# A transformer layer on one core: the first and last rounds written out by hand, the values' bias folded into the output bias, warm-up matmuls at the start

## What is computed

```python
def attn(x):                                   # after _layernorm(x)
    Q = jnp.einsum('btd,hkd->bthk', x, W_Q) + b_Q      # K, V alike
    scores = jnp.einsum('bqhk,bshk->bhqs', Q, K) / sqrt(d_head)
    attn = jax.nn.softmax(scores, axis=-1)
    out_h = jnp.einsum('bhqs,bshk->bqhk', attn, V)
    return jnp.einsum('bqhk,hdk->bqd', out_h, W_O) + b_O
def ffn(x):                                    # after _layernorm(x)
    gate = softmax(xt @ gate_w.T)
    base = xt @ weight.T
    t = jnp.einsum('nh,erh->ner', xt, lora_U)
    return base + jnp.einsum('ne,eor,ner->no', gate, lora_V, t) / 16
x = x + _layernorm(attn(_layernorm(x)))
x = x + _layernorm(ffn(_layernorm(x)))
```

## Time and profile before

| | us |
|---|---|
| median of 3 runs | 1220.18 (1218.62 to 1221.35) |
| the profiled execution's own time | 1221.85 |
| its span, first to last instruction | 1220.0 |
| granted TensorE clock, mean | 0.990 |
| PE busy | 1185.9 (97%) |
| DVE, ACT, POOL busy | 958.6, 967.9, 728.3 |

### The profile page before, as it was taken

The page is one execution under the profiler, slowest core; times in us unless marked ns, Lnnn a source line. Parts: engine busy times, 40 slices in busy tenths (PEclk is TensorE's granted clock), DMA queues, the critical chain, the costliest instruction groups (busy, mean ns, idle before and its releaser), DMA issues.

```text
span 1220.0 us, 32981 instructions
## 1 busy us (share of the span) xinstructions
PE 1185.9 (97%) x10532; PEld 977.1 (80%) x10532; DVE 958.6 (79%) x2618; ACT 967.9 (79%) x3079; POOL 728.3 (60%) x946
## 2 busy tenths in 40 slices
PE   6899999999999999999999999999999999999995
PEld 3688888888888888888888888888888888888883
DVE  4677888887888887887877878877888878788883
ACT  2678888888888888888888888888888888888882
POOL 2556556665556665566665666675556665555653
PEclk9899999999999999999999999999999999999997
DMA  6000000000000000000000000000000000000000
GB/s 213 2 1 6 2 6 4 4 4 4 0 4 4 4 4 4 0 4 4 4 4 4 4 0 4 4 4 4 4 0 4 4 4 4 4 0 4 4 4 9
DMA packets 9923, 10.95 MB, mean 9 GB/s; under 512 B 816, under 2 KB 9392, under 8 KB 9904
## 3 DMA queue, kind: packets, MB, share of 16 engines
q1 hardware_dynamic: 9904, 10.70, 2.7%
HBM read 6.50 MB, written 4.19 MB: 9 GB/s over the span
## 4 chain that ended last, share of the span: by engine, by line
PE 82%; POOL 7%; DVE 6%; issue 4%; ACT 1%; POOLq 0%; DVEq 0%; DMA 0%; SPq 0%; ACTq 0%
PE o_ps L383 17%; PE st_ps L365 17%; PE st_ps L355 14%; PE extra_ps L398 8%; PE qk_ps L304 4%; PE qk_ps L306 4%; PE qk_ps L305 4%; POOL probs L1021 3%; PE extra_ps L337 3%; PE extra_ps L339 2%; PE extra_ps L338 2%; DVE probs_t L806 2%; PE extra_ps L270 2%; POOL xn L1010 1%; POOL xn L1015 1%
## 5 line engine op out<-in xcount | busy, mean ns | idle before, releaser
L1021 POOL TENSOR_TENSOR probs<-probs,inv_sum 128x512 f32<-128x512 f32 x512 | 525.4, 1042 | 352.6 <-DVE inv_sum L801 342.0
L563 ACT ACTIVATE probs<-st_ps,neg_max 128x256 f32<-128x256 f32 x1024 | 475.2, 482 | 102.6 <-DVE neg_max L794 99.7
L794 DVE TENSOR_REDUCE neg_max<-st_ps 128x2 f32<-128x512 f32 x512 | 332.0, 680 | 48.8 <-PE st_ps L355 45.7
L365 PE MATMUL st_ps<-ident,probs 128*128 128x128 f32 x2048 | 286.6, 275 | 6.7 <-POOL probs L1021 5.1
L365 PEld LDWEIGHTS st_ps<-ident,probs 128*128 128x128 f32 x2048 | 233.9, 141 | 46.9 <-POOL probs L1021 21.6
L383 PE MATMUL o_ps<-probs_t,v_sb 128*64 128x256 f32 x2048 | 256.3, 387 | 0.3 <-DVE o_lo L812 0.2
L563 ACT ACTIVATION_READ_ACCUMULATOR probs<-st_ps,neg_max 128x1 f32 x1024 | 217.1, 212 | 0.0
L806 DVE COPY probs_t<-st_ps 128x512 f32<-128x512 f32 x256 | 169.4, 683 | 37.4 <-PE st_ps L365 37.3
L383 PEld LDWEIGHTS o_ps<-probs_t,v_sb 128*64 128x64 f32 x2048 | 133.4, 136 | 73.2 <-issue 5.9
L778 DVE TENSOR_TENSOR qk_lo<-qk_ps,qk_hi 128x512 fp32r<-128x512 f32 x256 | 175.1, 684 | 11.8 <-ACT qk_hi L550 11.5
L571 ACT COPY probs_t<-st_ps 128x512 f32<-128x512 f32 x256 | 152.5, 596 | 32.6 <-PE st_ps L365 32.6
(11 more groups left out here) (116 smaller groups left out, 2073.4 us busy)
## 6 DMA issues: line engine op xcount, KB each, us to landing
out<-x_all SPq DMA_DIRECT2D x32, 128.0 KB, 1.7
x_all<-in_x SPq DMA_DIRECT2D x1, 3840.0 KB, 17.3
stage_v<-in_w_v SPq DMA_DIRECT2D x1, 512.0 KB, 4.1
stage_o<-in_w_o SPq DMA_DIRECT2D x1, 512.0 KB, 6.7
stage_q<-in_w_q SPq DMA_DIRECT2D x1, 384.0 KB, 4.7
stage_k<-in_w_k SPq DMA_DIRECT2D x1, 384.0 KB, 5.8
x_all<-in_x SPq DMA_DIRECT2D x2, 128.0 KB, 3.1
ffn<-in_ffn_w SPq DMA_DIRECT2D x1, 196.0 KB, 6.8
```

Source lines behind the costliest of these rows:

```text
L365: last = nc.tensor.transpose(st_ps[p % 2][h][:, s * T + j * P:s * T + (j + 1) * P], probs[p % N_PROBS][h][:, j, s * P:(s + 1) * P], ident[ ...
L563: last = nc.scalar.activation(probs[n][h][:, j, :], st_ps[p % 2][h][:, j * T:(j + 1) * T], ACT.Exp, bias=neg_max[n][h][:, j:j + 1], accum_ ...
L794: nc.vector.tensor_reduce(neg_max[p % N_PROBS][h][:, :], st_ps[p % 2][h][:, :].rearrange("p (j s) -> p j s", j=NT), AX.X, ALU.max, negate= ...
L1021: nc.gpsimd.tensor_tensor(probs[n][h][:, :, :], probs[n][h][:, :, :], inv_sum[n][h][:, :].unsqueeze(2).to_broadcast([P, NT, T]), ALU.mult) ...
```

## The change

It has four parts.

1. `body` loses its `live` tests and is only used inside the loop, in the same order as before; `run` keeps only the loop. What body(0) to body(2) did before the loop, and body(32) and body(33) after it, is written out on every engine in a new order. Rounds 0 to 2 still reach the same point before the loop.
2. The bias of V is no longer put on the weights. W_V is used as loaded (pieces 2 and 3 of `MEANS` and the diagonals for v go away). Instead `ffn_means` multiplies W_V with a column of ones (8 matmuls of one column), DVE forms `v_offset`, and `output_bias` (9 matmuls of one column) carries it through W_O into the output bias.
3. PE runs 12 fp32 matmuls of 128 x 128 (`warm_up`) before its first real work.
4. ACT starts with a copy of one column (`seen_one`), so its table load comes early; stats_x(1) and stats_x(2) move to the front of DVE's list. The loads, and their order on SP, do not change.

```diff
+WARM_UPS = 12
@@ tensor @@
+            def warm_up():
+                for _ in range(WARM_UPS):
+                    nc.tensor.matmul(st_ps[1][1][:, 0:P], mean_w[:, :], mean_w[:, :], start=True, stop=True)
+            def ffn_means():
+                pe.wait_ge(mean_folded, 5)
+                pe.wait_ge(ffn_rows_centred, 1)
+                nc.tensor.matmul(o_ps[:, 0:D + TG], mean_w[:, :], ffn[:, F_W:F_W + D + TG],
+                                 start=True, stop=True)
+                pe.wait_ge(w_loaded["v"], 16)
+                for pair in range(PAIRS):
+                    last = nc.tensor.matmul(o_ps[:, D + TG + pair:D + TG + pair + 1],
+                                            stage["v"][:, pair_cols(pair)], one[:, 0:1],
+                                            start=True, stop=True)
+            def output_bias():
+                pe.wait_ge(v_offset_ready, 1)
+                pe.wait_ge(ffn_ready, 1)
+                pe.wait_ge(w_o_centred, 1)
+                dst = o_ps[:, D + TG + PAIRS:D + TG + PAIRS + 1]
+                nc.tensor.matmul(dst, neg_mean_w[:, :], bias[:, B_O:B_O + 1], start=True, stop=False)
+                for pair in range(PAIRS):
+                    last = nc.tensor.matmul(dst, stage["o"][:, pair_cols(pair)], v_offset[:, pair:pair + 1],
+                                            start=False, stop=(pair == PAIRS - 1))
@@ PE before the loop @@
+            warm_up()
+            weight_means(0)
+            transpose_xn(0)
+            weight_means(1)
+            weight_means(2)
+            project_v(0, 0, free=(xt_lo_ready, 1))
+            project_qk(0, 0)
+            project_qk(0, 1)
+            weight_means(3)
+            project_v(0, 1, free=(v_copied[0], 1))
+            weight_means(4)
+            scores(0, 0)
+            weight_means(5)
+            project_v(0, 2, free=(v_copied[1], 1))
+            ffn_means()
+            scores(0, 1)
+            transpose_probs(0, 0, 1, free=(exp_ready[1], 1))
+            project_qk(0, 2, free=(qk_lo_ready, 1))
+            project_qk(0, 3, free=(qk_lo_ready, 2))
+            output_bias()
+            transpose_probs(0, 0, 0, free=(exp_ready[0], 1))
...
+            project_qk(0, 7, free=(qk_lo_ready, 6))
+            probs_v(0, 0)
+            probs_v(0, 1)
+            transpose_probs(0, 2, 1, free=(exp_ready[1], 3))
+            transpose_probs(0, 2, 0, free=(exp_ready[0], 3))
+            transpose_probs(0, 3, 1, free=(exp_ready[1], 4))
...
+            scores(1, 0, free0=(probs_t_copied[0], 7), free1=(probs_t_copied[1], 7))
+            project_qk(1, 4, free=(qk_lo_ready, 11))
+            scores(1, 1, free0=(probs_t_copied[0], 8), free1=(probs_t_copied[1], 8))
+            project_qk(1, 5, free=(qk_lo_ready, 12))
+            probs_v(0, 6, free=(o_lo_ready, 3))
+            probs_v(0, 7)
+            transpose_probs(1, 0, 1, free=(exp_ready[1], 9))
+            transpose_probs(1, 0, 0, free=(exp_ready[0], 9))
+            transpose_probs(1, 1, 1, free=(exp_ready[1], 10))
...
+            scores(1, 5, free0=(probs_t_copied[0], 12), free1=(probs_t_copied[1], 12))
+            transpose_x1(0, free=(x1_ready, 1))
+            transpose_probs(1, 4, 0, free=(exp_ready[0], 13))
+            transpose_xn(2, free=(x1t_ready, 1))
+            transpose_probs(1, 4, 1, free=(exp_ready[1], 13))
+            project_qk(2, 0, free=(qk_lo_ready, 15))
...
+            probs_v(1, 6, free=(o_lo_ready, 7))
+            probs_v(1, 7)
+            transpose_probs(2, 0, 0, free=(exp_ready[0], 17))
+            output_projection(1, 0, free=(v_copied[2], 3))
...
+            transpose_probs(2, 3, 1, free=(exp_ready[1], 20))
+            scores(2, 4, free0=(probs_t_copied[0], 19), free1=(probs_t_copied[1], 19))
+            scores(2, 5, free0=(probs_t_copied[0], 20), free1=(probs_t_copied[1], 20))
+            transpose_x1(1, free=(x1_ready, 2))
+            transpose_probs(2, 4, 0, free=(exp_ready[0], 21))
@@ PE after the loop @@
             run(pe, 2, body)
+            transpose_probs(31, 4, 1, free=(exp_ready[1], 253))
+            probs_v(31, 2, free=(o_lo_ready, 125))
+            probs_v(31, 3)
+            transpose_probs(31, 5, 1, free=(exp_ready[1], 254))
+            project_tg(30, free=(x1t_ready, 31))
+            transpose_probs(31, 5, 0, free=(exp_ready[0], 254))
+            scores(31, 6, free0=(probs_t_copied[0], 253), free1=(probs_t_copied[1], 253))
+            probs_v(31, 4, free=(o_lo_ready, 126))
+            probs_v(31, 5)
+            scores(31, 7, free0=(probs_t_copied[0], 254), free1=(probs_t_copied[1], 254))
+            transpose_u(30, free=(u_ready, 31))
+            transpose_probs(31, 6, 1, free=(exp_ready[1], 255))
+            project_z(30, free=(ut_ready, 31))
+            transpose_probs(31, 6, 0, free=(exp_ready[0], 255))
+            output_projection(31, 0, free=(z_copied, 31))
+            transpose_probs(31, 7, 1, free=(exp_ready[1], 256))
+            output_projection(31, 1)
+            transpose_probs(31, 7, 0, free=(exp_ready[0], 256))
+            output_projection(31, 2)
+            probs_v(31, 6, free=(o_lo_ready, 127))
+            probs_v(31, 7)
+            output_projection(31, 3)
...
@@ DVE before the loop @@
+            stats_x(0)
+            norm_first_x()
+            stats_x(1)
+            stats_x(2)
+            fold_means(0)
+            weight_lo("v", every, w_hi_ready, w_lo_ready)
+            fold_means(1)
+            weight_lo("q", early, early_hi_ready, early_lo_ready)
+            xt_low(0)
+            weight_lo("k", early, early_hi_ready, early_lo_ready)
+            fold_means(2)
+            w_o_means()
+            centre_ffn_rows()
+            qk_lo(0, 0)
+            qk_lo(0, 1)
+            fold_means(3)
...
+            row_max(1, 4, 0)
+            row_max(1, 4, 1)
+            residual_x1(0)
+            invert_sum(1, 4, 0)
+            qk_lo(1, 7)
+            row_max(1, 5, 1)
+            invert_sum(1, 4, 1)
+            copy_x1t(0)
+            row_max(1, 5, 0)
+            stats_x1(0)
+            invert_sum(1, 5, 1)
+            attention_lo(1, 1)
+            xt_low(2)
...
@@ DVE after the loop @@
+            row_max(31, 4, 1)
+            row_max(31, 4, 0)
+            row_max(31, 5, 1)
+            row_max(31, 5, 0)
+            invert_sum(31, 4, 0)
+            residual_x1(30)
...
@@ ScalarE @@
+            nc.scalar.copy(seen_one[:, :], one[:, :])
+            weight_hi("v", every, w_hi_ready)
...
+            attention_hi(1, 3)
+            copy_v(2, 2)
```

More of the change, by code:

```diff
@@ new lines, in _ @@
+            output_projection(1, 1)
+            transpose_probs(2, 1, 0, free=(exp_ready[0], 18))
+            output_projection(1, 2)
+            output_projection(1, 3)
+            scores(2, 2, free0=(probs_t_copied[0], 17), free1=(probs_t_copied[1], 17))
+            scores(2, 3, free0=(probs_t_copied[0], 18), free1=(probs_t_copied[1], 18))
+            project_v(2, 3, free=(yt_ready, 2))
+            project_qk(2, 6, free=(qk_lo_ready, 21))
+            probs_v(2, 0, free=(o_lo_ready, 8))
@@ new lines, in _ @@
+            copy_yt(0)
+            exponentials(1, 2, 1)
+            exponentials(1, 2, 0)
+            exponentials(1, 3, 0)
+            exponentials(1, 3, 1)
+            copy_v(1, 3)
+            attention_hi(1, 0)
+            qk_hi(1, 6)
+            copy_probs_t(1, 2)
+            copy_probs_t(1, 3)
+            qk_hi(1, 7)
+            exponentials(1, 4, 0)
+            exponentials(1, 4, 1)
+            attention_hi(1, 1)
+            exponentials(1, 5, 1)
+            copy_probs_t(1, 4)
@@ new lines, in _ @@
+            xt_high(2)
+            exponentials(1, 5, 0)
+            qk_hi(2, 0)
+            gate_exponentials(0)
+            qk_hi(2, 1)
+            copy_probs_t(1, 5)
+            qk_hi(2, 2)
+            exponentials(1, 6, 0)
+            exponentials(1, 6, 1)
+            copy_v(2, 0)
+            exponentials(1, 7, 1)
+            exponentials(1, 7, 0)
+            copy_probs_t(1, 6)
+            copy_v(2, 1)
+            attention_hi(1, 2)
+            qk_hi(2, 3)
+            copy_ut(0)
@@ L687, in _ @@
+            attention_hi(31, 3)
+            copy_yt(31)
+            gate_exponentials(31)
+            copy_ut(31)
+            copy_z(31)
         @block.vector
@@ L727, in stats_x, with norm_first_x @@
                 ln_stats(LN_X, x_tiles(b), b + 1)
[L728 to L733 removed]
+            def norm_first_x():
+                dve.wait_ge(rstd_ready[LN_X], 1)
+                ln_apply(LN_X, xn, x_all).then_inc(xn_ready, 1)
             def xt_low(b):
@@ new lines, in _ @@
+            qk_lo(0, 1)
+            fold_means(3)
+            weight_lo("o", every, w_hi_ready, w_lo_ready)
+            fold_means(4)
+            weight_lo("q", late, w_hi_ready, w_lo_ready)
+            row_max(0, 0, 1)
+            fold_means(5)
+            row_max(0, 0, 0)
+            invert_sum(0, 0, 1)
+            weight_lo("k", late, w_hi_ready, w_lo_ready)
```

(15 more changed lines are left out.)

1053 lines of the change are left out of this document (657 added, 396 removed).

## The result

The changed kernel takes 1233.44 us (median of 4 runs, 1233.12 to 1235.95) against 1220.13 for the kernel before: a ratio of 1.0114, 95% interval 1.0097 to 1.0132. It is slower, as predicted, but by 13.3 us where 7.3 were predicted, and above the upper end of the range (1232).

A forecast was written before the change was run, and what follows sets the result against it. PE was taken to bound the kernel, busy 1054 of 1055 us in the loop. +6.85 before the loop and +0.4 at the end gave +7.3, so 1220.18 became 1227.5 us; 8-in-10 range 1218 to 1232.

The forecast's parts named there:

- The loop: The 29 loop rounds, 36.37 us each: order unchanged, so the change is worth nothing there.
- The load is waited for: Start: stats_x(2), moved forward on DVE, waits for the last load until 22.9; project_v(0,0) starts at 26.4.
- From there to transpose_probs(0,3,1): From 26.4 to the first full set of probabilities: 27.6 us of PE work, no waits, reaching 54.0.
- The round's own work: Between 26.4 and 54.0: PE's products of the round up to transpose_probs(0,3,1), at 0.11 each, 17.6 us.
- The half clock: After the load wait PE starts at half clock; three products of v and most of twelve of q, k cost 1.6 more.
- The 3.6 us of one-column products: Before 54.0: 17 products of ffn_means and output_bias at 0.21 us each add 3.6.
- the new start is 0.6 ahead: At transpose_probs(0,3,1): although it waits 13 us longer, the new start is 0.6 us ahead of the kernel before.
- From 54 to the loop: From 54.0 to the last step before the loop: 73.3 us of work plus 7.85 of waits, ending at 135.15.
- rival C: The clock also falls at waits before project_qk(2,0) and the loop, about 1.6 us each: 1230.7 with both; chance 0.15.
- The end: After the loop: 0.8 won on output_projection, but row_max order delays other steps; copy_yt starts 0.4 us later.
- A: From 54 to the loop PE finds its operands ready, without the predicted waits: 1219.6, no difference; chance 0.20.
- B: Start: the load is no wait or a shorter one; all moves 9.9 us earlier, 1217.6, faster; chance 0.10.

The follow-up runs named there:

- the early load: Changed kernel, but x of round 2 comes with that of round 1 in one early load: 1226.81 us, ratio 1.0057.
- the kernel with the statistics moved: Changed kernel with stats_x(2) moved behind qk_lo(0,5) on DVE and its rstd on GpSimd moved to match: 1219.78 us, ratio 0.9987.
- the best version found: Changed kernel, new order only for old body(0)'s steps; stats_x(1), its normalising and product 5's split placed as in the new order: 1211.19 us, ratio 0.9936.
- the kernel with one round new: Changed kernel with its new order only for the steps of old body(0), rounds 1 and 2 in the old order, new end: 1217.87 us, ratio 0.9975.

## Why the prediction was right in direction and too small

Two steps failed. The loop was put at nothing and cost 3.6 us in the profiled runs, and the work between 54 us and the loop was taken 4.3 us too small, of which 2.6 reached the entry of the loop. The wait that makes the kernel slower was right.

- **The load is waited for: right.** Predicted 22.9 and 26.4, measured 21.88 and 25.30. The load landed 1.0 earlier, the 3.5 us from there to the first product were 3.4. The 13.37 of the kernel before that the prediction sets beside it is its first product of queries and keys; its first value product comes at 25.09.
- **From there to transpose_probs(0,3,1): the point right, by luck in part.** Predicted 54.0; it starts at 54.0 to 54.1 (three sets of four transposes from 53.03 take 1.53). The round's own work is said to be 17.6, but its terms add up to 17.2, and with that the point would have been 53.6. The half clock lasted to 31 us and took some 2.7 us, not 1.6; the sum absorbed it with the earlier load. The 3.6 us of one-column products are in the trace (1.84 and 1.93 for their two rows of eight), but what they add to the time is nothing that two runs could find. That the new start is 0.6 ahead although it waits hid how much the new start can win: without the wait x of round 1 is transposed at 34.35 in place of 49.01.
- **From 54 to the loop: a step that failed.** Predicted 73.3 of work and 7.85 of waits, entry at 135.15; measured 83.77 (77.62 busy and 6.15 idle), entry at 137.77. The places of the waits were right: 2.49 before transpose_probs(2,4,0) with transpose_x1(1) (predicted 2.5), 0.6 before output_projection(1,0) (0.9), 0.85 before project_qk(2,0) and 0.66 in the two transposes ahead of it (2.3). The idle time shown is 6.15, less than predicted. What was mis-sized is the work, 77.6 in place of 73.3: it was taken at the 0.11 us of a product in a solid stretch, while each wait also lays bare the tail of the product before it. The products in front of the 13 waits show 3.7 us in all where 13 steps of 0.11 are 1.4; that is 2.3 of the 4.3, an estimate from the timeline, and the other 2.0 were not taken apart. And the chain of the prediction left out that GpSimd normalises x of round 3 before it scales the probabilities that PE waits for: they could be scaled from 136.3 on (the reciprocal starts at 136.14), and it starts at 136.67, so this is some 0.4 of the last wait of 0.84.
- **The loop: the term that was put at nothing.** "Worth nothing here" was wrong by 3.6 us. 2.2 are a fall of the clock behind the entry: rival C in mechanism (1.6 each). It had 0.15; the forecast left it out. It comes and goes with the same waits (2.2, 1.6, 1.6, 1.6 and 1.3 us in five kernels with this entry, none in two), so it is a cost of some runs, and its share in the median is open. 1.4 are the 0.05 us per round, which no step foresaw; their cause stays open.
- **The end: right in sign.** Predicted +0.4, measured +0.8. With 2.6 in front of the loop, 3.6 in it and 0.4 here, 6.6 of the 6.9 us that the sum lacked are named for the profiled runs. By the medians it lacked 6.0, and no trace of a median run divides these.
- **The rivals.** A (PE's idle time under 3 us from 54 on) is refuted by the 6.15. B's condition was built with the early load: the first product moved by 7.4, not 9.9, because norm_x(1) ends past 14, not at 13, and the load had landed 1.0 earlier. B and the forecast agreed on the mechanism, and the kernel with the statistics moved confirms it: that wait is the whole difference between the changed kernel and one that is level with the kernel before.

By runs, then: the wait for the last load costs 13.7 to 15.5 us, round 2's order with its entry into the loop 5.7, and against them stands what the new start of round 0 brings. Of the orders in front of the loop only round 0's is new in the best version found; with a mended seam it is 8.7 us faster than the kernel before by the medians of its group (1211.19 against 1219.93), and it is the best with either end (ratios 0.9936 and 0.9919). It also has the values' bias folded into the output bias, with two mean pieces of W_V less (3.4 us on PE before, by the prediction's rows) and fewer diagonals on GpSimd, and the warm-up. No run parts these from the order, so how much of the gain is the order's is open.

## What to carry to other kernels

A queue runs in order, so an item moved forward brings its guard with it: look up what the moved step waits for, when that lands, and what stands behind it on the same engine. One line cost more here than the whole rewriting gained. When a steady order and a hand-written one meet, look at the seam: the small steps that free a bank for the next product must not stand behind a chain that waits for another engine.

Price a wait from start to start of the products around it, and not by the idle time shown. And where leaving a part out moves no time, look in the trace for what took the gain: 14 of the one-column products looked like 2.9 us of PE's time, without them two rounds came 1.6 us sooner, and a stretch at half clock took most of it back.

## What the runs showed of the hardware that was not expected

The clock can fall in an idle stretch or only behind it, and it does not always fall. In the long wait of the changed kernel it is at 0.90 from 12 to 14 us and at 0.50 from 14 on, with PE idle until 25.30. In the kernel with one round new PE is idle from 34 to 38 us with the clock at 1.00, and at 0.61 when it works again; windows of PE:

```profile
34.00:38.00 4.00, 0.00 (x0) 1.00 0.00 0
38.00:42.00 4.00, 3.45 (x16) 0.61 0.02 6
```

With the seam mended and either end, PE's longest waits from 34 to 60 us are the same (1.2 for GpSimd, 0.7, and 0.2 for ACT), yet the clock stays at 1.00 in the profiled run with the new end:

```profile
42.00:46.00 4.00, 2.78 (x24) 1.00 0.00 0
```

and falls in the one with the old end:

```profile
44.00:46.00 2.00, 1.89 (x8) 0.50 0.00 0
46.00:48.00 2.00, 2.00 (x14) 0.65 0.00 0
```

Each such stretch lasts three to seven us and takes half of that; that is the size of the 2 to 4 us by which runs of one kernel differ, though only the profiled runs show the clock by time.

The start varies in the same way. The kernel before with the new end has the same start as the kernel before, and in its profiled run the fourth mean product looks like this:

```profile
10.50 1.06 PE L275 MATMUL st_ps<-stage_k,neg_mean_w 128*128 128x256 f32 x2
```

The first product of queries and keys, at 13.44, takes 0.55. In the kernel before the two take 0.81 and 0.35: there the full clock had come by 11 us, here not yet at 13.
